# One feed-forward slab in a scratch place, the narrow layer's split halves in other places, and the fourth graph layer's logits ahead of its low halves

## The chip, the cores and the metric

The kernel runs as one program on one core of a Trainium2 chip. The metric is the device time of one execution in microseconds. The engines are PE (matrix products), DVE and ACT (elementwise work), POOL, and SP, which issues nearly all loads of weights.

## The reference

The input is 128 nodes of 768 numbers and 2048 edges. Eight blocks follow each other, each adding to its input what it computes from a normalised copy:

```
x = x + L0_gnn(layernorm(x))   # attention over edges: 8 heads x 768, then 1 x 768
x = x + L0_ffn(layernorm(x))   # tokens split by a router: self-attention or mixing; then a 48-wide net
x = x + L1_gnn(layernorm(x))   # 8 heads x 128, relu, then 1 x 768
x = x + L1_ffn(layernorm(x))   # mixture: 8 experts + 1 shared, 1536 wide, 2 chosen per token
x = x + L2_gnn(layernorm(x))   # 12 heads x 64
x = x + L2_ffn(layernorm(x))   # 8 experts, 48 wide
x = x + L3_gnn(layernorm(x))   # 4 heads x 512, elu, then 1 x 768
x = x + L3_ffn(layernorm(x))   # mixture: 8 experts, 3072 wide, 2 chosen per token
```

A graph layer projects x, forms for each edge a logit from two terms per head, takes a softmax over each node's incoming edges, and sums the projected neighbours by it.

## The kernel before

**Slabs and places.** All large weights lie in memory as slabs of 128 x 3072 numbers (1.5 MB). SP issues one load a slab (L596), in a fixed order, into one of 15 places: six in `ring` (0 to 5), six in `scratch` (6 to 11), three in `extra` (12 to 14). The table `SLOT` says which slab goes where; until the first mixture it is the slab's number modulo 6, after that the place that is given up first. Before each load SP waits (`room`) for the semaphore that tells that the place's former slab is used up (`when_used`). SP is one queue: a load that waits holds up all behind it.

**The slabs around the change.** Slabs 24 to 31 belong to L0_ffn: in order the weights of keys, queries, values, mixing (to 29) and attention output (four of its six tiles in 30, two in 31), and in 31 also those of the 48-wide net. 32 to 35 are the four slabs of the L1 graph layer (`c` = 2 in the code, the "narrow" layer), and 36 onward are the first mixture's: nine for the shared expert, then those of the chosen experts, which SP can only address once the router has written their order (`sid`, L634). The first nine of the second mixture are loaded ahead of its router in the same way.

**Split products.** Most weights are multiplied as a rounded high half and a rest: ACT writes the high half (`narrow_split_hi`, `graph_split_hi`), DVE subtracts it (`narrow_split_lo`, `graph_split_lo`), each in two pieces of 128 x 1536, and PE multiplies both. ACT and DVE run their instructions in the order in which the program has them.

**The stretch of L0_ffn.** PE forms the logits of self-attention; DVE takes their maximum (`self_max`); ACT takes exponentials (L993); DVE normalises (`self_weights`); PE transposes (L2235), runs two more parts of the mixing product (L2209), and multiplies by the values (L2243); ACT copies the context (L1001); PE forms `attn_out` (L2252), which ends in `merged` (L2258).

**The narrow layer.** Two segments of 512 columns pass through `project`, `term_rows`, `logits`, `weights_of`, `turn_attention`, `attend`, `activate`, `turn_segment` (L1779) and `product2` (L1811), with step t of each engine's loop `first_narrow(2)` working on different segments at once.

**The fourth graph layer** (`c` = 5) runs the same loop over four segments. POOL loads its attention vectors (`vectors`) when an earlier pair of vectors has been used, and `terms` on DVE waits for them. Ahead of it, in L2_ffn, ACT takes a Gelu (L1039) of PE's product L2333, and DVE weights the result (L1614).

Of the kernel before, what the change touches and what calls it, by code (L numbers as in the profile page):

```python
# [19 lines left out]
RING = 6  # L20
# [36 lines left out]
FFN0_SLAB = 24  # L57
# [116 lines left out]
for k, s in enumerate(slots_in_turn(1, [0, 1, 14, 2, 7, 3, 8, 4, 9, 6, 5, 12])):  # L174
    SLOT[MOE[1]["slab"] + k] = s
# [131 lines left out]
def gnn_ffn_kernel(nc, x_in, edges_in, weights, rows_in, cols_in, small_in, attn_in, ffn0_vectors, l2_terms_in, out):  # L307
    with ExitStack() as ctx:
# [283 lines left out]
        def _(sp):  # L592
            sp.dma_start(X[:], x_in).then_inc(S("x_loaded"), 16)

            def slab(n, index):
                sp.dma_start(slab_at(n), weights[index]).then_inc(land[SLOT[n]], 16)  # L596
# [54 lines left out]
            for n in range(MOE[1]["slab"]):  # L651
                room(n)
                slab(n, n)
# [82 lines left out]
        def _(act):  # L736
# [131 lines left out]
            def first_narrow(c):  # L868

                n = FIRST[c]["segs"]  # L870
                for t in range(n + 3):
                    if c == 2 and t < 2:
                        narrow_split_hi(t + 2)
# [115 lines left out]
            narrow_split_hi(0)  # L989
# [5 lines left out]
            ins.then_inc(S("self_exps"), 1)  # L995
            act.wait_ge(S("self_turned"), 1)
            A(ALT[:, 0:3 * P], TP[:, 0:3 * P], ACT.Copy).then_inc(S("self_attn_ready"), 1)
            act.wait_ge(S("places_turned"), 1)
            A(placesT, MS[:, 2 * P:3 * P], ACT.Copy).then_inc(S("places_ready"), 1)
            act.wait_ge(S("context"), 1)  # L1000
# [7 lines left out]
            narrow_split_hi(1, (1,))  # L1008
            transposed(3)
            act.wait_ge(S("f_product"), 1)  # L1010
            A(FT[0:F0, :], MS[0:F0, 0:P], ACT.Gelu, bias=cols[0:F0, 14:15]).then_inc(S("f_ready"), 1)

# [24 lines left out]
            graph_split_hi(1)  # L1037
# [4 lines left out]
            A(CBT[0:E8, :], TP[0:E8, SEG:SEG + P], ACT.Copy).then_inc(S("l2_T_ready"), 1)  # L1042
            keep_x(6)
# [10 lines left out]
        def _(dve):  # L1054
# [259 lines left out]
            def first_narrow(c):  # L1314
                n, k, C = FIRST[c]["segs"], GAT[c]["group"], GAT[c]["C"]
                for t in range(n + 2):
                    if c == 5 and t == 5:
                        graph_segment_lo(2)
                    if c == 2 and t == 0:
                        narrow_split_lo(2)  # L1320
                    if c == 2 and t == 2:
                        narrow_split_lo(3, (0,))
                    if c == 5 and t < 3:
                        graph_split_lo(*((2, (0,)), (3, (0,)), (3, (1,)))[t])
                    if 0 <= t - 1 < n:
                        logits(c, t - 1)
                    if t < n:
                        dve.wait_ge(S("h_copied"), SEG_BASE[c] + t + 1)
                        terms(GAT[c]["unit"] + t, range(t * k, t * k + k), C, h_tile(c, t))
                        if c == 5 and t == 0:  # L1330
                            graph_split_lo(2, (1,))
# [5 lines left out]
                    if c == 2 and t == 2:  # L1337
                        narrow_split_lo(3, (1,))
# [247 lines left out]
            narrow_split_lo(1, (1,))  # L1586

# [890 lines left out]
```

## Time and profile before

| | before |
|---|---|
| time of the runs | 1204.87 us median of 3 (1202.83 to 1208.21) |
| time of the profiled execution | 1205.36 us |
| its span, first to last instruction | 1203.6 us |
| PE busy | 1142.2 us (95%) |
| DVE busy | 581.8 us (48%) |
| ACT busy | 458.5 us (38%) |
| bytes moved by DMA | 443.15 MB, mean 368 GB/s |
| mean granted clock of PE | 0.994 |

The span runs from the first instruction to the last; the time of an execution holds 1.8 us around it. Busy shares are means over stages with different limits. The granted clock is a share of full speed (2.4 GHz).

### The profile page before, as it was taken

What the parts mean: (1) busy time and instruction counts of PE and PEld (TensorE: products, weight loads), DVE (VectorE), ACT (ScalarE), POOL (GpSimd) and SP (SyncE); (2) the same over time, 40 slices, a digit from 0 to 9 for tenths busy, and PEclk for the clock granted to TensorE, in tenths of its full rate; (3) what the DMA queues carried; (4) which work ended last, traced back from release to release, by engine and by line L of the source; (5) the groups of instructions that cost most, each with busy time, mean ns of one, the idle gap of its engine ahead of it and who ended that gap; (6) DMA issues with size and microseconds to landing.
All of it is one profiled execution on the core that took longest, in us unless ns stands there. A gap on an engine that the chain in (4) does not pass through costs nothing.

```text
span 1203.6 us, 15702 instructions
## 1 busy us (share of the span) xinstructions
PE 1142.2 (95%) x6347; PEld 721.7 (60%) x6347; DVE 581.8 (48%) x892; ACT 458.5 (38%) x525; POOL 22.4 (2%) x48
## 2 busy tenths in 40 slices
PE   8899998989999999989999999999999999889988
PEld 6677784767855455535866686565665655445533
DVE  7877742747644234301665684454554543223410
ACT  4755613515633223201444364343443432222210
POOL 2000010000000000000000000000000000000000
PEclk9999999989999999999999999999999999999999
DMA  9998564864999999999786298999999999999997
GB/s 372 423 407 344 199 246 180 337 266 192 426 425 426 424 425 425 426 420 419 290 311 260 82 428 337 427 425 427 425 424 425 426 426 424 425 426 425 425 423 285
DMA packets 45368, 443.15 MB, mean 368 GB/s; under 512 B 5088, under 2 KB 5248, under 8 KB 11888
## 3 DMA queue, kind: packets, MB, share of 16 engines
q1 hardware_dynamic: 42336, 427.05, 85.5%
q0 software_dynamic: 2960, 15.09, 3.3%
q8 instruction: 51, 0.84, 0.3%
q14 instruction: 21, 0.17, 0.0%
HBM read 441.73 MB, written 0.39 MB: 367 GB/s over the span
## 4 chain that ended last, share of the span: by engine, by line
PE 70%; DMA 14%; ACT 5%; SPq 5%; DVE 4%; issue 1%; POOL 0%; DVEq 0%; ACTq 0%
PE PJ L2036 14%; PE PJ L2005 10%; DMA scratch<-in_weights 9%; PE AC L2073 8%; PE TP L2095 6%; PE PJ L2014 5%; DMA ring<-in_weights 5%; SPq L647 4%; PE AC L1832 3%; PE AC L1820 2%; PE PJ L1996 2%; PE TP L2046 2%; PE MS L1633 1%; PE PJ L1766 1%; PE AC L1811 1%
## 5 line engine op out<-in xcount | busy, mean ns | idle before, releaser
L2036 PE MATMUL PJ<-ring,picked 128*64 128x512 f32 (+1 forms) x588 | 149.7, 594 | 0.0
L915 ACT ACTIVATE low<-PJ 128x512 f32<-128x512 f32 x51 | 30.3, 593 | 242.8 <-PE PJ L2036 170.2
L1391 DVE SCALAR_TENSOR_TENSOR act<-low,CB,PJ 128x512 f32<-128x512 f32 x51 | 38.0, 746 | 159.4 <-PE PJ L2005 84.1
L2036 PE MATMUL PJ<-scratch,picked 128*32 128x512 f32 (+1 forms) x360 | 106.9, 594 | 2.2 <-DMA extra<-in_weights 2.2
L2095 PE MATMUL TP<-ring,extra 128*64 128x512 f32 (+3 forms) x384 | 102.5, 488 | 2.8 <-issue 2.4
L1409 DVE TENSOR_TENSOR ring_lo<-ring,w_lo_u 128x1536 fp32r<-128x1536 f32 x40 | 69.2, 1756 | 52.4 <-ACT w_lo_u L932 52.4
L2095 PE MATMUL TP<-scratch,extra 128*64 128x512 f32 (+3 forms) x320 | 86.5, 489 | 0.4 <-DMA ring<-in_weights 0.4
L932 ACT ACTIVATE w_lo_u<-ring 128x1536 fp32r<-128x1536 f32 x40 | 58.3, 1487 | 66.6 <-DMA ring<-in_weights 30.2
L2036 PEld LDWEIGHTS PJ<-ring,picked 128*64 128x64 f32 (+1 forms) x588 | 42.7, 124 | 55.6 <-issue 54.9
L1409 DVE TENSOR_TENSOR ring_lo<-ring,w_hi_u 128x1536 fp32r<-128x1536 f32 x34 | 58.9, 1755 | 23.4 <-ACT w_hi_u L932 23.2
L2014 PE MATMUL PJ<-ring_lo,XTh 128*128 128x512 f32 x168 | 67.2, 400 | 0.0
L932 ACT ACTIVATE w_hi_u<-scratch 128x1536 fp32r<-128x1536 f32 x26 | 37.5, 1482 | 77.6 <-DMA scratch<-in_weights 61.8
L2095 PE MATMUL TP<-extra 128*64 128x256 f32 (+3 forms) x256 | 64.4, 488 | 0.9 <-issue 0.9
L932 ACT ACTIVATE w_hi_u<-ring 128x1536 fp32r<-128x1536 f32 x34 | 49.7, 1487 | 29.9 <-PE AC L2073 20.1
L2005 PE MATMUL PJ<-w_lo_u,extra_lo 128*128 128x512 f32 x150 | 60.6, 404 | 0.0
L2005 PE MATMUL PJ<-w_hi_u,extra_lo 128*128 128x512 f32 x150 | 58.9, 403 | 1.7 <-DVE extra_lo L1409 1.7
L2005 PE MATMUL PJ<-w_lo_u,XTh 128*128 128x512 f32 x150 | 59.2, 395 | 0.0
L2005 PE MATMUL PJ<-w_hi_u,XTh 128*128 128x512 f32 x150 | 59.2, 394 | 0.0
L2095 PEld LDWEIGHTS TP<-ring,extra 128*64 128x64 f32 (+1 forms) x384 | 38.2, 124 | 34.4 <-issue 29.1
L2036 PE MATMUL PJ<-extra,picked 128*32 128x512 f32 (+1 forms) x204 | 58.9, 594 | 0.0
L2036 PE MATMUL PJ<-ring,extra 128*64 128x512 f32 x156 | 53.5, 595 | 3.0 <-DMA ring<-in_weights 2.2
L2073 PE MATMUL AC<-w_hi_u,extra_lo 128*128 128x512 f32 x208 | 48.9, 348 | 6.0 <-DVE extra_lo L1417 6.0
(467 smaller groups left out, 2256.0 us busy)
## 6 DMA issues: line engine op xcount, KB each, us to landing
ring<-in_weights SPq DMA_DIRECT2D x147, 1536.0 KB, 17.6
scratch<-in_weights SPq DMA_DIRECT2D x73, 1536.0 KB, 19.6
extra<-in_weights SPq DMA_DIRECT2D x39, 1536.0 KB, 20.7
extra<-in_attn POOLq DMA_DIRECT2D x11, 768.0 KB, 10.7
ring<-in_weights SPq DMA_DIRECT2D x8, 768.0 KB, 30.1
extra<-in_attn POOLq DMA_DIRECT2D x6, 512.0 KB, 10.7
extra<-in_weights SPq DMA_DIRECT2D x4, 768.0 KB, 25.7
ring<-in_weights SPq DMA_DIRECT2D x8, 384.0 KB, 16.8
```

The source lines that it names most:

```text
L647: sp.dma_start(slab_at(of)[:, part], weights[index, :, part]) \
L915: A(silu, PJ[:, 0:SEG], ACT.Silu).then_inc(S("silu_ready"), 1)
L932: A(hi_half(n, half), half_slab(n, half), ACT.Copy).then_inc(S("whole_hi"), 1)
L1391: v.scalar_tensor_tensor(hexp, silu, weight, PJ[:, SEG:2 * SEG], ALU.mult, ALU.mult) \
L1409: v.tensor_tensor(slab_lo(n)[:, half * HALF:(half + 1) * HALF], half_slab(n, half), hi_half(n, half).bitcast(F32), ALU.subtract).then_inc( ...
L1820: ins = mm(AC[:, a:b], act1T[:, j % 2, t * P:(t + 1) * P], slab_at(n)[:, t * D + a:t * D + b], start=(j == 0 and t == 0), stop=(j == last ...
L1832: ins = mm(AC[:, a:b], x[:, t * P:(t + 1) * P], w[:, t % 2 * D + a:t % 2 * D + b], start=(j == 0 and t == 0 and x is xl), stop=False, skip ...
L2005: return mm(dst, x[:, t, :], hi_half(n, t // 3)[:, t % 3 * SEG:(t % 3 + 1) * SEG], start=start, stop=stop)
L2014: mm(dst, XTh[:, t, :], slab_lo(n)[:, t * SEG:(t + 1) * SEG], start=(apart and t == 0), stop=False)
L2036: ins = mm(dst[c], x[:, t, c], slab_at(LOAD[q, kind, side])[:, t * SEG:(t + 1) * SEG], start=(t == 0), stop=(t == KT - 1))
L2073: ins = mm(AC[:, a:b], x[:, t * P:(t + 1) * P], w[:, a:b], start=False, stop=(q == end and t == 3 and w is hi and x is hTh), skip_group_ch ...
L2095: ins = mm(Y[c, a:b], hT_of(q)[:, t * P:(t + 1) * P][:, c], slab_at(LOAD[q, "d", side])[:, t * D + a:t * D + b], start=(j == j0 and t == 0 ...
```

## The change

The kernel's diff has four parts. First, slab 30 (`CONTEXT_SLAB`) goes to place 6, the first sixth of `scratch`, which the first graph layer gives up when its last segment has been multiplied (`segment_product` at 12). The slabs behind it move back by one place: 31 to place 0, 32 to 1, 33 to 2, 34 to 3, 35 to 4, 36 to 5. So SP now waits before slab 31 for `k_product` (before: `q_product`), before 32 for `q_product` (as before), before 33 for `q_product` (before: `v_product`), before 34 for `v_product` (before: `merged`), and before 35 for `merged` (as before). The first mixture takes up its places in another opening order, since place 5 is now in its list first; the events that its loads wait for are the same, under other place numbers. Of the slabs 117 to 126, behind it, slabs 118, 120, 122 and 124 now wait for the next later of the last passes' products.

Second, ACT's narrow high halves stand elsewhere: slab 32's halves behind the exponentials, slab 34's halves inside L0_ffn (before: in the narrow layer). Third, DVE's low halves of slabs 34 and 35 stand earlier by up to two steps. Fourth, one high half of slab 120 moves behind ACT's Gelu, and in the fourth graph layer the two low halves of its fourth slab stand behind `logits`.

```diff
@@ -171,7 +171,11 @@
 
 
 SLOT = {n: n % RING for n in range(MOE[1]["slab"])}
-for k, s in enumerate(slots_in_turn(1, [0, 1, 14, 2, 7, 3, 8, 4, 9, 6, 5, 12])):
+CONTEXT_SLAB = FFN0_SLAB + 6
+SLOT[CONTEXT_SLAB] = 6
+for n in range(CONTEXT_SLAB + 1, MOE[1]["slab"]):
+    SLOT[n] = (n - 1) % RING
+for k, s in enumerate(slots_in_turn(1, [5, 0, 1, 14, 2, 7, 3, 8, 4, 9, 6, 12])):
     SLOT[MOE[1]["slab"] + k] = s
 free = []
 for n in range(L2_SLAB - 1, MOE[1]["slab"], -1):
@@ -650,6 +654,8 @@
 
             for n in range(MOE[1]["slab"]):
                 room(n)
+                if n == CONTEXT_SLAB:
+                    sp.wait_ge(S("segment_product"), FIRST[0]["segs"])
                 slab(n, n)
             mixture(1, (8, 9), 14, 12)
             for n in range(L2_SLAB, MOE[3]["slab"]):
@@ -869,8 +875,8 @@
 
                 n = FIRST[c]["segs"]
                 for t in range(n + 3):
-                    if c == 2 and t < 2:
-                        narrow_split_hi(t + 2)
+                    if c == 2 and t == 0:
+                        narrow_split_hi(3)
                     if c == 5 and t < 2:
                         graph_split_hi(t + 2, (0,))
                     if t < n:
@@ -986,17 +992,18 @@
             ins.then_inc(S("mix_ready"), 1)
             act.wait_ge(S("v_product"), 1)
             A(V, AC[:, 0:D], ACT.Copy).then_inc(S("v_ready"), 1)
-            narrow_split_hi(0)
             act.wait_ge(S("self_max"), 1)
             for r, s, at in ((slice(0, P), 0, SEG), (slice(0, P), 1, 2 * SEG), (slice(0, DH), 2, SEG + P),
                              (slice(DH, P), 2, 2 * SEG + P)):
                 ins = A(EE[r, s * P:(s + 1) * P], TP[r, at:at + P], ACT.Exp, bias=hneg[r, s:s + 1], scale=DH ** -0.5,
                         accum_out=hsum[r, s:s + 1])
             ins.then_inc(S("self_exps"), 1)
+            narrow_split_hi(0, (0,))
             act.wait_ge(S("self_turned"), 1)
             A(ALT[:, 0:3 * P], TP[:, 0:3 * P], ACT.Copy).then_inc(S("self_attn_ready"), 1)
             act.wait_ge(S("places_turned"), 1)
             A(placesT, MS[:, 2 * P:3 * P], ACT.Copy).then_inc(S("places_ready"), 1)
+            narrow_split_hi(0, (1,))
             act.wait_ge(S("context"), 1)
             A(contextT.rearrange("p k n -> p (k n)"), AC[:, 0:D // 4], ACT.Copy).then_inc(S("context_ready"), 1)
             narrow_split_hi(1, (0,))
@@ -1006,9 +1013,11 @@
                 r = slice(c * BLOCK, (c + 1) * BLOCK)
                 A(spread[r, c * (D // 4):(c + 1) * (D // 4)], MS[r, 0:D // 4], ACT.Copy).then_inc(S("spread_made"), 1)
             narrow_split_hi(1, (1,))
+            narrow_split_hi(2, (0,))
             transposed(3)
             act.wait_ge(S("f_product"), 1)
             A(FT[0:F0, :], MS[0:F0, 0:P], ACT.Gelu, bias=cols[0:F0, 14:15]).then_inc(S("f_ready"), 1)
+            narrow_split_hi(2, (1,))
 
             keep_x(2)
             transposed(4, XTh[:])
@@ -1034,12 +1043,13 @@
             transposed(7)
             act.wait_ge(S("pe_d"), LAST_PASS[1] + 1)
             graph_split_hi(0)
-            graph_split_hi(1)
+            graph_split_hi(1, (0,))
             act.wait_ge(S("l2_hidden_product"), 1)
             A(G2, PJ[:, 0:E8 * F2], ACT.Gelu).then_inc(S("l2_gelu"), 1)
             act.wait_ge(S("l2_turned"), 1)
             A(G2T, TP[:, 0:E8 * F2], ACT.Copy).then_inc(S("l2_T_ready"), 1)
             A(CBT[0:E8, :], TP[0:E8, SEG:SEG + P], ACT.Copy).then_inc(S("l2_T_ready"), 1)
+            graph_split_hi(1, (1,))
             keep_x(6)
 
             transposed(8, XTh[:])
@@ -1317,13 +1327,16 @@
                     if c == 5 and t == 5:
                         graph_segment_lo(2)
                     if c == 2 and t == 0:
-                        narrow_split_lo(2)
-                    if c == 2 and t == 2:
+                        narrow_split_lo(2, (1,))
                         narrow_split_lo(3, (0,))
-                    if c == 5 and t < 3:
-                        graph_split_lo(*((2, (0,)), (3, (0,)), (3, (1,)))[t])
+                    if c == 2 and t == 1:
+                        narrow_split_lo(3, (1,))
+                    if c == 5 and t == 0:
+                        graph_split_lo(2, (0,))
                     if 0 <= t - 1 < n:
                         logits(c, t - 1)
+                    if c == 5 and 1 <= t < 3:
+                        graph_split_lo(3, (t - 1,))
                     if t < n:
                         dve.wait_ge(S("h_copied"), SEG_BASE[c] + t + 1)
                         terms(GAT[c]["unit"] + t, range(t * k, t * k + k), C, h_tile(c, t))
@@ -1334,8 +1347,6 @@
                         narrow_segment_lo(t - 2)
                     if 0 <= t - 1 < n:
                         weights_of(c, t - 1)
-                    if c == 2 and t == 2:
-                        narrow_split_lo(3, (1,))
                     if 0 <= t - 2 and FIRST[c]["elu"]:
                         activate(c, t - 2)
                     if c == 5 and 3 <= t < 5:
@@ -1584,6 +1595,7 @@
             dve.wait_ge(S("h1_ready"), 1)
             layernorm_affine(2, H1[:], vec(3), vec(4))
             narrow_split_lo(1, (1,))
+            narrow_split_lo(2, (0,))
 
             layernorm(3, X[:], 5, 2)
             transposed_lo(4, XT_lo, "graph_tokens_lo")
```

On ACT, in L0_ffn, from the copy of the values (`scratch<-AC 128x768`) to the activation that ends L0_ffn, the rows before are these. L865 is a high half of a narrow slab (`extra_lo` is slab 32's, `w_lo_d` slab 33's, `w_hi_g` slab 34's), L993 the exponentials, L997 to L1007 the copies of attention, places, context and output.

```order
L988 ACTIVATE scratch<-AC 128x768
L865 ACTIVATE extra_lo<-ring 128x1536 x2
L993 ACT_TABLE_LOAD
L993 ACTIVATE scratch,hsum<-TP,hneg 128x128 x2
L993 ACTIVATE scratch,hsum<-TP,hneg 64x128 x2
L997 ACTIVATE scratch<-TP 128x384
L999 ACTIVATE scratch<-MS 128x128
L1001 ACTIVATE scratch<-AC 128x192
L865 ACTIVATE w_lo_d<-ring 128x1536
L1007 ACTIVATE scratch<-MS 32x192 x2
L865 ACTIVATE w_lo_d<-ring 128x1536
L743 ACTIVATE extra<-TP 128x384 x2
```

And in the change, where L871 is the high half and L998 the exponentials:

```order
L994 ACTIVATE scratch<-AC 128x768
L998 ACT_TABLE_LOAD
L998 ACTIVATE scratch,hsum<-TP,hneg 128x128 x2
L998 ACTIVATE scratch,hsum<-TP,hneg 64x128 x2
L871 ACTIVATE extra_lo<-ring 128x1536
L1003 ACTIVATE scratch<-TP 128x384
L1005 ACTIVATE scratch<-MS 128x128
L871 ACTIVATE extra_lo<-ring 128x1536
L1008 ACTIVATE scratch<-AC 128x192
L871 ACTIVATE w_lo_d<-ring 128x1536
L1014 ACTIVATE scratch<-MS 32x192 x2
L871 ACTIVATE w_lo_d<-ring 128x1536
```

Slab 32's two halves stand behind the exponentials, one of them ahead of the copies and one behind, and the next row of the change is slab 34's first half.

On DVE, in the narrow layer's third step (t = 2), L1166 to L1169 normalise the weights of segment 0, L1240 is the first low half of slab 35, and L1147 opens the logits of segment 1. Before:

```order
L1166 TENSOR_SCALAR hsum<-hsum 128x4
L1168 RECIPROCAL hrec<-hsum 128x4
L1169 TENSOR_TENSOR scratch<-scratch,hrec 128x512
L1240 TENSOR_TENSOR ring_lo<-ring,w_lo_g 128x1536
L1147 ISA scratch,hmax<-TP,maskb 128x128
L1147 ISA hmax 128x1
```

And in the change, where L1176 to L1179 and L1157 are the same lines:

```order
L1176 TENSOR_SCALAR hsum<-hsum 128x4
L1178 RECIPROCAL hrec<-hsum 128x4
L1179 TENSOR_TENSOR scratch<-scratch,hrec 128x512
L1157 ISA scratch,hmax<-TP,maskb 128x128
L1157 ISA hmax 128x1
```

The low half (`ring_lo<-ring,w_lo_g`) no longer stands between the two; it stands at the loop's first and second step.

On ACT, in L2_ffn, L859 writes the high halves of slabs 119 (`w_hi_u`) and 120 (`w_lo_u`), L1039 is the Gelu, and L1041 and L1042 copy its transposed result. Before:

```order
L743 ACTIVATE extra<-TP 128x384 x2
L859 ACTIVATE w_hi_u<-ring 128x1536 x2
L859 ACTIVATE w_lo_u<-scratch 128x1536 x2
L1039 ACT_TABLE_LOAD
L1039 ACTIVATE scratch<-PJ 128x384
L1041 ACTIVATE scratch<-TP 128x384
L1042 ACTIVATE scratch<-TP 8x128
```

And in the change, where L865 is the high half and L1048 the Gelu:

```order
L749 ACTIVATE extra<-TP 128x384 x2
L865 ACTIVATE w_hi_u<-ring 128x1536 x2
L865 ACTIVATE w_lo_u<-scratch 128x1536
L1048 ACT_TABLE_LOAD
L1048 ACTIVATE scratch<-PJ 128x384
L1050 ACTIVATE scratch<-TP 128x384
L1051 ACTIVATE scratch<-TP 8x128
L865 ACTIVATE w_lo_u<-scratch 128x1536
```

Slab 120's second half has moved from ahead of the Gelu to behind the copies.

## Rows read from the trace of the kernel before

**Rows 1.** The page: 40 slices of 30.1 us; shares of the last chain.
```profile
GB/s 372 423 407 344 199 246 180 337 266 192 426 425 426 424 425 425 426 420 419 290 311 260 82 428 337 427 425 427 425 424 425 426 426 424 425 426 425 425 423 285
...
PE 70%; DMA 14%; ACT 5%; SPq 5%; DVE 4%; issue 1%; POOL 0%; DVEq 0%; ACTq 0%
```

**Rows 2.** Waits of SP's DMA queue: us, times, longest.
```profile
SPq L634 <- DVE sid L1435: 52.9, 2, 31.2
```

**Rows 3.** Timeline of SP's queue: start, us, instruction.
```profile
262.63 23.48 SPq L596 DMA_DIRECT2D scratch<-in_weights  x2
...
684.36 0.88 SPq L596 DMA_DIRECT2D ring<-in_weights  x2
```

**Rows 4.** Timeline of ACT: start, us, instruction [idle before <- releaser].
```profile
168.11 1.28 ACT L977 ACT_TABLE_LOAD   x1
...
194.20 2.86 ACT L865 ACTIVATE extra_lo<-ring 128x1536 fp32r<-128x1536 f32 x2 [1.95 <-DMA ring<-in_weights]
197.07 1.28 ACT L993 ACT_TABLE_LOAD   x1
```

**Rows 5.** Timeline of DVE, 193 to 201.
```profile
193.16 0.17 DVE L1570 TENSOR_SCALAR hneg<-hmax 128x3 f32<-128x3 f32 x1
200.01 0.18 DVE L1572 RECIPROCAL hrec<-hsum 128x3 f32<-128x3 f32 x1 [6.69 <-ACT scratch L993]
```

**Rows 6.** Timeline of PE, 191 to 207.
```profile
191.94 4.14 PE L2209 MATMUL PJ<-ring,scratch 128*128 128x512 f32 x12
...
200.84 0.90 PE L2235 MATMUL TP<-ident,scratch 128*128 128x128 f32 x3 [4.65 <-DVE scratch L1573]
201.53 3.96 PE L2209 MATMUL PJ<-ring,scratch 128*128 128x512 f32 x8
```

**Rows 7.** Landings: slabs 31 (issued 181.6), 32 (182.0), vector loads (150.9, 151.4).
```profile
DMA to landing us min/median/max: 8.5/8.5/8.5
DMA to landing us min/median/max: 12.2/12.2/12.2
DMA to landing us min/median/max: 8.8/11.3/13.8
```

**Rows 8.** Windows: width, busy by engine, PEclk, DMA share, GB/s.
```profile
201.00:204.00 3.00, 3.00 (x7) 1.88 (x8) 3.00 (x2) 0.66 (x2) 0.00 (x0) 0.51 0.02 5
245.20:251.40 6.20, 5.51 (x18) 4.43 (x19) 4.25 (x13) 1.18 (x3) 0.00 (x0) 0.50 0.53 223
256.00:261.00 5.00, 3.58 (x21) 2.98 (x22) 1.28 (x2) 0.60 (x1) 0.00 (x0) 1.00 1.01 430
```

**Rows 9.** The chain by time, narrow layer: start, us, what.
```profile
240.95 1.67 DVE ring_lo L1240
...
244.47 0.60 DVE act L1184
...
246.92 6.66 PE AC L1811 x24
...
258.05 4.52 PE AC L1811 x24
```

**Rows 10.** Timeline of PE, 242 to 246.
```profile
242.35 1.16 PE L1766 MATMUL PJ<-scratch 128*128 128x128 f32 x8 [0.26 <-ACT scratch L790]
245.11 1.12 PE L1779 MATMUL MS<-ident,act 128*128 128x128 f32 x4 [1.61 <-DVE act L1184]
```

**Rows 11.** Timeline of ACT, at 599.
```profile
598.81 1.28 ACT L1039 ACT_TABLE_LOAD   x1
```

**Rows 12.** Timeline of DVE, 596 to 631.
```profile
596.58 3.43 DVE L1225 TENSOR_TENSOR ring_lo<-ring,w_hi_u 128x1536 fp32r<-128x1536 f32 x2
600.63 0.56 DVE L1614 TENSOR_TENSOR scratch<-scratch,extra 128x384 f32<-128x384 f32 x1 [0.62 <-ACT scratch L1039]
...
630.60 0.69 DVE L1128 CUSTOM_DVE_ANT_0 extra<-scratch,extra 128x512 f32<-128x512 f32 x1 [1.00 <-DMA extra<-in_attn]
```

**Rows 13.** Timeline of PE, 595 to 599.
```profile
594.97 4.14 PE L2333 MATMUL PJ<-ring,extra 128*128 128x384 f32 x12
```

## The prediction

> **What bounds the kernel now.** I read the page first. Its slices of 30.1 us show weights streaming at about 425 GB/s from 300 to 570 us and, but for one slice, from 690 us to the last; between 90 and 300, and again between 570 and 690, the rate is 82 to 344 GB/s [rows 1]. The chain that ended last runs mostly over PE (70%), but that is because products free the places for loads; at full rate the bytes set the pace. The waits of SP's queue then say why a stream starts when it does: it stood 52.9 us in two waits for the order of the experts [rows 2], that is for each mixture's router. Both streams start from an idle DMA: the slices holding the two waits have 192 and 82 GB/s [rows 1]. So what the compute ahead of a router gains moves the whole stream behind it, PE with it, and the end. Nothing that changes inside a mixture is part of this change: the loads wait for the same products there, under other place numbers. The first load past the order goes out at 262.63 + 23.48 = 286.1 in the first mixture and at 684.4 in the second [rows 3]. So the sum is made of what is gained ahead of 286, and between the first mixture's last product and 684.
>
> **L0_ffn.** DVE has the maximum at 193.16 + 0.17 = 193.33 [rows 5], but ACT waits for slab 32 to land until 194.20, writes its high halves until 197.06, loads the exponential's table for 1.28 [rows 4], and its exponentials end at about 200.0, where DVE's reciprocal starts [rows 5]. PE, whose work before ended 4.65 earlier, resumes at 200.84 [rows 6]. In the change the table load comes right behind the copy of the values. ACT was idle for 1.95 before 194.20 [rows 4], so it is free at 192.25, the table is in at 193.53, and everything up to PE's transposes comes 197.07 + 1.28 - 193.53 = 4.8 earlier. PE itself is busy until 200.84 - 4.65 = 196.19, so 4.65 is the gain, and the gap closes.
>
> That gap also cost clock. In the window behind it the granted clock is 0.51, the lower level of 1.2 GHz [rows 8]; three transposes take 0.69 to the next start there and eight products of the mixing weight 3.96. At the upper level, 2.4 GHz, twelve such products take 4.14 [rows 6], so eight take 2.76, and the transposes half of theirs, 0.35: a gain of 1.2 + 0.35, of which I take 1.5. **L0_ffn: 4.65 + 1.5 = 6.15 less.**
>
> What must hide: half of slab 32's high half (1.43, half of 2.86) stands between the exponentials (then ending at 195.2) and the copy of attention. That copy is queued behind it, and PE waits for the copy only after its eight products, at about 199.3; so slab 32 may land as late as 197 at no cost. It is third in the queue now and took 12.2 from 182.0, to 194.2; in the change it is second, as slab 31 now, which took 8.5 from 181.6, to 190.1 [rows 7]. Behind it, slabs 33 and 34 take the turns of 32 and 33. The halves of 34 that now stand in L0_ffn (three pieces, two on ACT and one on DVE) fall into stretches where these engines wait for PE; if that cover were gone, each would cost its 1.4 to 1.8.
>
> Slab 30 now loads earlier, beside the vector loads of L0_ffn, the later of which is issued at 151.4 and lands 13.8 later, at 165.2 [rows 7]. ACT's table load for the router's sigmoid waits for it and stood at 168.11 [rows 4]. 1.57 MB at 425 GB/s are 3.7, so it could land at 168.9 at worst: 0 to +0.8. I take 0, since slab 30 queues behind another slab and shares only the last part.
>
> **The narrow layer.** The chain has DVE write a low half from 240.95 for 1.67, then the logits, then the activation at 244.47 [rows 9]. Without that half the logits can end 1.67 earlier, but the activation also waits for the product L1766, which ends at 242.35 + 1.16 = 243.51 [rows 10]. It starts at about 243.6: **-0.85**, and PE's wait before L1779 shrinks from 1.61 [rows 10] to about 0.75. The half itself moves to DVE's wait for PE ahead of the first logits; were there no wait, 1.67 would come back.
>
> From that wait on the clock is 0.50 until 251.4 [rows 8]: four transposes take 1.12 [rows 10], and the following product 6.66 against 4.52 for its like at full clock [rows 9]. If the clock holds, 0.55 and 2.15 are gained: **-2.7**; if it falls again, 0. I take -2.7: the stretch at 256 to 261, with PE busy 3.58 of 5.00, keeps 1.00 [rows 8], and it holds the same sequence of product, activation and transposes for the other segment, with shorter waits, which is what the change makes of the first.
>
> The Trainium skill speaks against that certainty ("TensorE: Matmul & The Clock Gate", Part 1): the clock is reduced by default and released by activity, judged in windows that run free of the program, so that a gap's effect depends on where it falls. Of the two low stretches here each follows a wait of PE, which agrees; by the rule a shorter gap may still be caught, the sum would lack 2.7, and that is rival A below.
>
> **L2_ffn and the fourth graph layer.** ACT writes two slabs' high halves and then loads the Gelu's table at 598.81 [rows 11]. One half less (1.43, as above) lets the load start at 597.4. The Gelu then waits for PE's product, which ends at 594.97 + 4.14 = 599.1 [rows 13], and DVE's weighting, at 600.63, for a low half that ends at 596.58 + 3.43 = 600.0 [rows 12]: **-0.6**, with a bound of 0 (if the table load stays behind) and -1.4. In the fourth graph layer the logits come one half (1.7) earlier, but the third `terms` starts at 630.60 on the landing of a vector load [rows 12], which is triggered by earlier `terms` that don't move. What the half gives back before is waited for there: **0** (bounds: 0 and -1.7, a half's length). The half that is now later has to be ready for PE's fourth projection; DVE's wait of 1.00 before 630.60 [rows 12] is there for it.
>
> Slabs 118, 120, 122 and 124 wait for a later product, but load while the stream drains and are needed after 590: 0.
>
> **Sum:** 6.15 + 0.85 + 2.7 + 0.6 = 10.3. The profiled execution took 1205.4 with a span of 1203.6, and stands 0.5 above the median of the runs (1204.9). **Prediction: 1195.0 us.**
>
> **The rivals.**
> A. The clock falls again in the narrow layer. For it: the wait there doesn't vanish. Then 10.3 - 2.7 = 7.6, 1197.8 us.
> B. Only L0_ffn's gain arrives; narrow layer and L2_ffn are held by something that the chain doesn't show (ACT's exponentials, a landing), and the change doesn't do there what it says. For it: both gains are small differences of ends that lie close together. Then 6.15, 1199.2.
> C. ACT's queue is held by slab 32. Its first half now stands ahead of the copy of attention; each microsecond that it lands past 197 is one of the path. It takes back all at a landing at 207.3 and makes the kernel 6 slower (1211) at 213. Against it: the longest of the landings in that stretch, as third in the queue, was 12.2 [rows 7]; here it would have to be 31.
> D. The gain ahead of the first router is lost in the mixture: 1204 at most. Against it: the DMA is idle before the wait ends [rows 1, 2].
>
> **How the numbers follow.** Forecast 0.60, A 0.20, B 0.11, D 0.05, C 0.04. What separates this kernel from no change is about 0.5%, 6 us, since its runs spread from 1202.8 to 1208.2. Forecast and A lie below 1198.8, so does B in half of its cases: faster 0.84. D and B's other half: same 0.12. C: slower 0.04. The range: below, -10.3 with 1.7 more in the fourth graph layer and 0.8 in L2_ffn, and the spread of runs, 1191.5; above, past B with 0.8 for the vector load, 1200.5. It leaves out C, D and the ends, under 2 in 10.
>
> **What would show it.** PE's wait of 4.65 gone and `self_exps` ahead of slab 32's halves; the granted clock at 1.00 from 190 to 260; L1811 twice at about 4.5; the first router's order about 9.7 earlier, at 276; the end of the first mixture as much; the Gelu's result 0.6 nearer to the mixture's end; the third `terms` still waiting for the vector load. The prediction is wrong if the first stream starts 9.7 earlier but doesn't end so, or if a new wait of ACT for a landing stands in L0_ffn.

## The result, and the profile after

The changed kernel took 1196.96 us (median of 4 runs, 1195.55 to 1199.68), the kernel before 1204.7 beside it (4 runs, 1202.83 to 1208.21): a ratio of 0.9935, 95% interval 0.9906 to 0.9964. Two more comparisons of the same two kernels, among the experiments below, give 1196.91 to 1206.7 (ratio 0.992, 0.9897 to 0.9944) and 1195.67 to 1205.31 (0.9925, 0.9908 to 0.9943). So it is faster by 0.65 to 0.8%, 7.7 to 9.8 us. Forecast were 10.3 and 1195.0, range 1191.5 to 1200.5. The profiled execution took 1199.68 with a span of 1197.9; of its four runs it is the slowest.

L0_ffn first. PE's timeline in the changed kernel, from the mixing product to the merged one (start, us, instruction, idle before):

```profile
192.03 4.14 PE L2221 MATMUL PJ<-ring,scratch 128*128 128x512 f32 x12
196.01 0.27 PE L2244 MATMUL MS<-ident,scratch 128*128 128x128 f32 x1
196.12 0.55 PE L2247 MATMUL TP<-ident,scratch 128*128 128x128 f32 x3
196.50 2.75 PE L2221 MATMUL PJ<-ring,scratch 128*128 128x512 f32 x8
...
204.74 1.53 PE L2270 MATMUL PJ<-scratch 128*128 128x512 f32 x4 [0.96 <-DVE scratch L1590]
```

L2247 are the transposes that waited 4.65 before [rows 6]: no wait stands there now, they take 0.55 for 0.90, and the eight products behind them 2.75 for 3.96. ACT's timeline shows why:

```profile
192.35 1.28 ACT L998 ACT_TABLE_LOAD   x1
...
195.28 1.49 ACT L871 ACTIVATE extra_lo<-ring 128x1536 fp32r<-128x1536 f32 x1
196.79 0.49 ACT L1003 ACTIVATE scratch<-TP 128x384 f32<-128x384 f32 x1
197.18 0.27 ACT L1005 ACTIVATE scratch<-MS 128x128 f32<-128x128 f32 x1
197.34 1.49 ACT L871 ACTIVATE extra_lo<-ring 128x1536 fp32r<-128x1536 f32 x1
```

The table load starts 4.7 earlier than in [rows 4], and slab 32's halves fill ACT's time behind the exponentials without a wait for a landing. The chain of the narrow layer in order of time comes next, then PE's wait in it, then windows (width, five busy times, PE's granted clock, DMA share, GB/s):

```profile
237.29 0.70 DVE act L1194
237.99 0.04 issue
238.04 0.67 PE MS L1791 x4
...
239.38 4.51 PE AC L1823 x24
...
248.36 4.51 PE AC L1823 x24
```

PE's wait ahead of the four transposes at 238.04 is 0.79, for 1.61 before [rows 10]:

```profile
238.04 0.66 PE L1791 MATMUL MS<-ident,act 128*128 128x128 f32 x4 [0.79 <-DVE act L1194]
```

```profile
201.00:204.00 3.00, 2.78 (x51) 1.65 (x49) 0.15 (x1) 1.04 (x2) 0.00 (x0) 1.00 0.00 0
238.00:245.00 7.00, 6.03 (x33) 4.74 (x33) 2.58 (x12) 1.20 (x2) 0.00 (x0) 1.00 0.70 276
245.00:252.00 7.00, 5.42 (x32) 4.55 (x33) 1.38 (x2) 0.60 (x1) 0.00 (x0) 1.00 0.92 388
...
528.00:532.00 4.00, 4.00 (x14) 1.43 (x12) 0.00 (x0) 0.00 (x0) 0.00 (x0) 0.57 1.02 418
586.00:590.00 4.00, 4.00 (x8) 2.19 (x8) 3.76 (x10) 3.90 (x3) 0.00 (x0) 0.57 0.00 0
```

The first of the two equal products took 6.66 before [rows 9] and takes 4.51 now; the low clock of [rows 8] is gone from both places. But two other places have one, 528 and 586, where the profiled execution of before had 1.00. SP's timeline has the two ends that the prediction named, the first loads past the routers' orders:

```profile
276.06 0.94 SPq L600 DMA_DIRECT2D scratch<-in_weights  x2
...
676.82 0.88 SPq L600 DMA_DIRECT2D ring<-in_weights  x2
```

Past the first order the load goes out 9.7 earlier than in the profiled execution of before (whose row in [rows 3] covers two loads; the second is at 285.76), as forecast. Past the second it is 7.5 earlier [rows 3], and the spans differ by 5.7 only. SP's waits for the orders are as long as they were [rows 2]:

```profile
SPq L638 <- DVE sid L1446: 53.0, 2, 31.2
```

So the mechanism came as predicted, and in this execution 4 of the 9.7 went astray behind 276. The experiments ask which of the steps ahead of 276 carry the gain, and whether the change lost those 4 or chance did.

### The profile page after: what moved, and what is told of

Its sections match the earlier page's. It is cut to its first block, busy times and chain, and to the rows that moved or that the text cites. A ratio compares the mean times of both kernels' runs of the same rounds, so it can differ in the third digit from the quotient of the medians.

```text
span 1197.9 us, 15702 instructions
## 1 busy us (share of the span) xinstructions
PE 1142.2 (95%) x6347; PEld 721.3 (60%) x6347; DVE 582.3 (49%) x892; ACT 458.3 (38%) x525; POOL 22.4 (2%) x48
## 4 chain that ended last, share of the span: by engine, by line
PE 73%; DMA 16%; ACT 4%; DVE 3%; SPq 3%; issue 1%; POOL 0%; DVEq 0%; ACTq 0%
PE PJ L2048 14%; PE PJ L2017 10%; DMA scratch<-in_weights 8%; PE AC L2085 8%; PE TP L2107 7%; PE PJ L2026 5%; DMA ring<-in_weights 4%; PE AC L1844 3%; DMA extra<-in_weights 3%; PE AC L1832 2%; SPq L651 2%; PE PJ L2008 2%; PE MS L1645 2%; PE TP L2058 2%; PE PJ L1778 1%
## 5 line engine op out<-in xcount | busy, mean ns | idle before, releaser
L2048 PE MATMUL PJ<-ring,picked 128*32 128x512 f32 (+1 forms) x612 | 160.4, 594 | 0.0
L2048 PE MATMUL PJ<-scratch,picked 128*64 128x512 f32 (+1 forms) x336 | 113.9, 600 | 2.2 <-DMA extra<-in_weights 2.2
L1420 DVE TENSOR_TENSOR ring_lo<-ring,w_lo_u 128x1536 fp32r<-128x1536 f32 x44 | 76.1, 1755 | 69.1 <-ACT w_lo_u L938 69.1
L2107 PE MATMUL TP<-ring,extra 128*64 128x512 f32 (+2 forms) x464 | 102.1, 488 | 0.9 <-issue 0.9
L2048 PEld LDWEIGHTS PJ<-ring,picked 128*32 128x32 f32 (+1 forms) x612 | 45.8, 123 | 58.6 <-issue 57.4
L938 ACT ACTIVATE w_hi_u<-scratch 128x1536 fp32r<-128x1536 f32 x30 | 43.5, 1483 | 76.5 <-DMA scratch<-in_weights 53.1
L2107 PE MATMUL TP<-extra 128*64 128x512 f32 (+2 forms) x224 | 64.3, 488 | 0.0
L2107 PEld LDWEIGHTS TP<-ring,extra 128*32 128x32 f32 (+1 forms) x464 | 38.9, 123 | 35.5 <-issue 30.6
L1420 DVE TENSOR_TENSOR ring_lo<-ring,w_hi_u 128x1536 fp32r<-128x1536 f32 x28 | 48.4, 1756 | 21.8 <-ACT w_hi_u L938 21.5
L938 ACT ACTIVATE w_hi_u<-ring 128x1536 fp32r<-128x1536 f32 x28 | 40.6, 1486 | 33.2 <-PE AC L2085 17.2
```

The costliest lines, as they stand in the source:

```text
L938: A(hi_half(n, half), half_slab(n, half), ACT.Copy).then_inc(S("whole_hi"), 1)
L1420: v.tensor_tensor(slab_lo(n)[:, half * HALF:(half + 1) * HALF], half_slab(n, half), hi_half(n, half).bitcast(F32), ALU.subtract).then_inc( ...
L2048: ins = mm(dst[c], x[:, t, c], slab_at(LOAD[q, kind, side])[:, t * SEG:(t + 1) * SEG], start=(t == 0), stop=(t == KT - 1))
L2107: ins = mm(Y[c, a:b], hT_of(q)[:, t * P:(t + 1) * P][:, c], slab_at(LOAD[q, "d", side])[:, t * D + a:t * D + b], start=(j == j0 and t == 0 ...
```

## The experiments

**Theory:** what the change gains ahead of the first order moves everything behind it; what is missing behind 276 are falls of the clock and delays of transfers that differ from one execution to the next, whatever the kernel. **Rival:** the change pays behind 550, by other places, the moved half of slab 120 and later waits; then the losses recur in each execution of it.

Below, "the order" is the order of the experts that a router writes, and a "fall" is a stretch in which the granted clock is at the lower level, 0.50 of full speed; a window that holds more than the fall shows a mean between 0.50 and 1.00.

All traces are set side by side in this table, worked out from PE's and SP's rows of each: end of the merged product (L0_ffn); from there to the first load past the first order (narrow layer and router); to the product that opens L2_gnn (mixture 1); the hidden product of L2_ffn; from its end to the transposes behind the Gelu; from there to the first load past the second order (the last of L2_ffn, fourth graph layer, router); from there to the end (mixture 2). The stretch between mixture 1 and the hidden product is left out: 32.35 to 32.61 in all.

| trace | merged ends | narrow | mixture 1 | hidden | to transposes | graph 4 | mixture 2 | span |
|---|---|---|---|---|---|---|---|---|
| before | 212.51 | 73.25 | 276.84 | 4.14 | 2.14 | 83.12 | 519.2 | 1203.6 |
| before_again | 211.61 | 72.15 | 278.01 | 5.49 | 1.17 | 84.38 | 519.4 | 1204.8 |
| narrow_warm | 212.44 | 71.70 | 277.76 | 5.52 | 1.17 | 84.39 | 520.8 | 1206.4 |
| order_only | 206.90 | 72.15 | 276.90 | 5.83 | 1.17 | 82.97 | 520.3 | 1198.6 |
| slots_only | 209.04 | 69.81 | 276.98 | 4.14 | 1.43 | 82.69 | 519.9 | 1196.3 |
| lo_at_2 | 206.39 | 71.89 | 277.70 | 5.53 | 1.17 | 82.68 | 521.0 | 1199.0 |
| no_l2 | 206.02 | 69.77 | 277.73 | 4.14 | 2.13 | 84.40 | 519.0 | 1195.6 |
| after | 206.27 | 69.79 | 277.74 | 5.83 | 1.17 | 83.65 | 521.1 | 1197.9 |
| after_again | 206.37 | 69.78 | 276.71 | 4.14 | 1.43 | 84.33 | 519.4 | 1194.5 |
| after_third | 206.26 | 69.76 | 276.84 | 4.14 | 1.43 | 82.79 | 520.0 | 1193.6 |
| warm_more | 206.47 | 69.77 | 277.07 | 4.14 | 1.43 | 83.36 | 521.2 | 1195.8 |

**after_again and before_again: both kernels once more.** No edit.

> The changed kernel once more, for a second trace. Theory (a shift that chance events eat into): the first load past the first router's order again at 276 us and the last product of the first mixture 9 to 10 earlier than before, but the stretches of low granted clock stand elsewhere than at 528, 586, 1078 and 1146, and the span differs from 1197.9 by 2 to 4. Median 1196 to 1197. Rival (the change itself costs something behind 550: other places, the moved half, other products): the low stretches and the losses of 0.9, 0.7, 0.5 and 1.8 stand at the same places again, span 1197.5 to 1198.5.

> The kernel before once more, for a second trace. Forecast's reason (the low clock at 245 to 251 follows from the wait of 1.6 there): the granted clock is 0.50 there again, the product behind it takes 6.7, the first load past the router's order goes out at 286. Rival (the fall is chance): the clock holds, the product takes 4.5, the order is known 2.7 earlier, at 283, and 2.7 of the change's gain isn't the change's.

The changed kernel: 1196.91 (6 runs, 1196.28 to 1199.41), order at 276.15, span 1194.5. The clock held where it had fallen, and fell at 616 to 622 instead:

```profile
586.00:590.00 4.00, 4.00 (x13) 2.25 (x12) 3.86 (x6) 3.45 (x4) 0.00 (x0) 1.00 0.00 0
528.00:532.00 4.00, 4.00 (x20) 1.38 (x16) 0.00 (x0) 0.00 (x0) 0.00 (x0) 1.00 1.02 418
616.00:622.00 6.00, 5.66 (x16) 3.47 (x16) 4.97 (x18) 3.30 (x6) 0.87 (x2) 0.72 0.94 376
```

The kernel before took 1206.61 in its one run. Its clock fell in the narrow layer again, but for less of it:

```profile
201.00:204.00 3.00, 3.00 (x7) 1.52 (x5) 2.09 (x2) 0.05 (x1) 0.00 (x0) 0.53 0.03 5
244.00:252.00 8.00, 7.09 (x33) 5.87 (x33) 4.41 (x14) 1.49 (x5) 0.00 (x0) 0.79 0.45 189
```

The order came at 283.76 and not 285.76: 1.1 from the shorter fall, and 0.9 since slab 32 landed earlier, which ACT's row shows (194.20 in [rows 4]):

```profile
193.18 2.86 ACT L865 ACTIVATE extra_lo<-ring 128x1536 fp32r<-128x1536 f32 x2 [1.18 <-DMA ring<-in_weights]
```

283.76 is near the rival's 283, but the rival's condition, a clock that holds, was not met.

For the rival's losses: in the table mixture 1 is 1 longer in 5 traces, of both kernels, each with a fall that starts between 526.9 and 535.9; so it is with the hidden product (1.4 to 1.7 longer), again in both. None of these losses comes back in each execution of the changed kernel, so the rival falls.

**order_only: the order on ACT alone**, on the kernel before, all places as before.

```diff
-            narrow_split_hi(0)
             act.wait_ge(S("self_max"), 1)
...
             ins.then_inc(S("self_exps"), 1)
+            narrow_split_hi(0, (0,))
...
             A(placesT, MS[:, 2 * P:3 * P], ACT.Copy).then_inc(S("places_ready"), 1)
+            narrow_split_hi(0, (1,))
```

> The kernel before with one edit: slab 32's high halves behind the exponentials, all places as before. Theory: the order alone does it, since slab 32 lands at 194.2 and its half is wanted at 195.2: PE's wait of 4.65 is gone, the merged product ends 6.2 earlier, the first order 6.2 earlier (279.6) if the narrow layer's wait stays as it was; median 1198 to 1199. Rival (the place is needed, the half waits for a landing): the first order within 2 us of 286, median over 1202.

1199.83 (6 runs, 1199.02 to 1201.82; ratio 0.9942, 0.9919 to 0.9965). PE has no wait ahead of the transposes, and ACT none ahead of slab 32's first half:

```profile
196.64 0.27 PE L2233 MATMUL MS<-ident,scratch 128*128 128x128 f32 x1
196.75 0.55 PE L2236 MATMUL TP<-ident,scratch 128*128 128x128 f32 x3
```

```profile
195.91 1.49 ACT L865 ACTIVATE extra_lo<-ring 128x1536 fp32r<-128x1536 f32 x1
```

The merged product ends 4.7 to 5.6 earlier than in the three traces with the old order, and L0_ffn started 0.6 later here (the mixing product at 192.67 for 192.03), behind a fall at 46.7 that the other traces lack. The narrow layer keeps its wait of 1.60 and a fall of the clock (72.15):

```profile
239.51 0.66 PE L1780 MATMUL MS<-ident,act 128*128 128x128 f32 x4 [1.60 <-DVE act L1185]
```

The order on ACT carries all of L0_ffn's gain.

**slots_only: the places alone.** The changed kernel with that edit undone.

```diff
             ins.then_inc(S("self_exps"), 1)
-            narrow_split_hi(0, (0,))
...
+            narrow_split_hi(0)
             act.wait_ge(S("self_max"), 1)
```

> The changed kernel with slab 32's high halves back ahead of the exponentials; the places stay changed. Theory (the order carries the gain, the place does little for it): slab 32 lands at 190.0, ACT writes its halves from 192.25 to 195.1, the table load ends at 196.4 and the exponentials at 198.1 instead of 195.2; PE waits 2.9 again, the clock may fall behind it as before (1.5), and the first load past the first router's order goes out at 279 to 280.5 instead of 276.1; median 3 to 4.4 above the changed kernel's. Rival (the earlier landing is what gives the gain): no wait of PE, 276 to 277, median within 1.

1199.13 (6 runs, 1198.16 to 1200.99; ratio 0.9935, 0.9919 to 0.9951). ACT no longer waits for the slab, but its halves still stand ahead of the table load, and PE waits 2.58:

```profile
192.26 2.85 ACT L871 ACTIVATE extra_lo<-ring 128x1536 fp32r<-128x1536 f32 x2
195.12 1.28 ACT L999 ACT_TABLE_LOAD   x1
```

```profile
198.89 0.55 PE L2246 MATMUL TP<-ident,scratch 128*128 128x128 f32 x3 [2.58 <-DVE scratch L1583]
```

The first load past the order goes out at 278.86, 2.8 behind the changed kernel's: the exponentials' delay, and no fall of the clock behind this shorter wait. What the places give, by the traces, is slab 34 early (landed at 200.3 in after, at 219.1 in before), so that three of its four halves can leave the narrow layer. That is argued and not shown: no run takes back the places alone.

**lo_at_2: slab 35's low halves back at the third step**, on the changed kernel.

```diff
-                        narrow_split_lo(3, (0,))
-                    if c == 2 and t == 1:
-                        narrow_split_lo(3, (1,))
+                    if c == 2 and t == 2:
+                        narrow_split_lo(3, (0,))
...
                         weights_of(c, t - 1)
+                    if c == 2 and t == 2:
+                        narrow_split_lo(3, (1,))
```

> The changed kernel with slab 35's low halves back at the narrow loop's third step. Forecast's reason (logits later by a half and a wait long enough for the clock to fall): the activation 0.85 later, PE's wait about 1.6, the product behind it at 6.6 instead of 4.5, the first load past the order at 276.1 + 0.85 + 2.7 = 279.6, median 3.5 above the changed kernel's. Rival (the clock falls by chance, not by that wait): 0.85 alone, 276.9, median 0.9 above.

1198.91 (6 runs, 1198.17 to 1200.78), 2.0 above after_again in the same comparison; ratio 0.9931, 0.9908 to 0.9953. The wait of 1.6 is back, the transposes start 0.81 later behind the merged product (238.97 - 206.39 against 238.04 - 206.27), and the clock falls:

```profile
238.97 0.66 PE L1792 MATMUL MS<-ident,act 128*128 128x128 f32 x4 [1.60 <-DVE act L1194]
```

```profile
236.00:244.00 8.00, 5.50 (x25) 4.62 (x26) 6.45 (x26) 2.03 (x6) 0.00 (x0) 0.79 0.79 335
```

The order is 2.2 later (278.28): 0.8 by the wait, 1.3 by the clock, for which 2.7 stood in the expectation. Between the theories it decides for the forecast's reason, at half its size.

**narrow_warm: the clock alone.** The kernel before, with fills in PE's wait.

```diff
                     if 0 <= t - 3 < n:
+                        if n == 2 and t == 3:
+                            keep_warm(13)
                         turn_segment(c, t - 3)
```

> The kernel before with 13 products of the identity, whose result nobody reads, in PE's wait of 1.6 ahead of the narrow layer's first transposes. Theory (the clock falls there because PE stands idle): the granted clock stays 1.00 from 245 to 252, the four transposes take 0.66 and the first product 4.5, the activation is as late as before, and the first load past the order goes out 2.7 earlier, at 283.1; median 2 to 3 below the kernel before. Rival (the fall is chance or follows from something else): 0.50 stands there again, 284 to 286, and the median is that of before.

The clock held, the product took 4.5, and the fills (two rows for each product) ended 1.1 behind the activation:

```profile
243.25 3.07 PE L1633 MATMUL MS<-ident 128*128 128x128 f32 x26
246.16 0.60 PE L1779 MATMUL MS<-ident,act 128*128 128x128 f32 x4
```

```profile
244.00:252.00 8.00, 7.31 (x51) 6.50 (x51) 5.18 (x17) 1.87 (x5) 0.00 (x0) 1.00 0.57 239
```

Narrow takes 71.70, so 70.6 but for the fills' delay; 2.65 less than in the first trace of before, 1.55 less than in the second. The time, 1206.14 (12 runs, 1202.54 to 1208.29; ratio 0.9987, 0.9971 to 1.0002), shows no sure gain, where 2 to 3 were expected: of the 1.55 to 2.65 that the fills win they give back 1.1.

**no_l2: without the fourth part.**

```diff
             graph_split_hi(0)
-            graph_split_hi(1, (0,))
+            graph_split_hi(1)
...
-            graph_split_hi(1, (1,))
...
-                    if c == 5 and t == 0:
-                        graph_split_lo(2, (0,))
+                    if c == 5 and t < 3:
+                        graph_split_lo(*((2, (0,)), (3, (0,)), (3, (1,)))[t])
                     if 0 <= t - 1 < n:
                         logits(c, t - 1)
-                    if c == 5 and 1 <= t < 3:
-                        graph_split_lo(3, (t - 1,))
```

> The changed kernel without its fourth part (both high halves of slab 120 ahead of the Gelu, the fourth graph layer's low halves ahead of its logits). Theory: from the end of the hidden product to PE's next transposes 2.1 again instead of 1.2, so 0.9 later from there on; in the fourth graph layer nothing, since its third terms wait for the vector load in either order; median 0.9 above the changed kernel's. Rival (the part is without effect, or harmful through the moved halves): 1.2 stays or is given back before the second router's order; median the same or lower.

1197.57 (6 runs, 1196.81 to 1199.3; ratio 0.9922, 0.9906 to 0.9938). ACT's table load ends behind the hidden product again, and PE waits:

```profile
585.88 4.14 PE L2342 MATMUL PJ<-ring,extra 128*128 128x384 f32 x12
592.15 0.55 PE L2349 MATMUL TP<-ident,scratch 128*128 128x128 f32 x3 [0.84 <-DVE scratch L1623]
```

```profile
589.72 1.28 ACT L1048 ACT_TABLE_LOAD   x1
591.01 0.49 ACT L1048 ACTIVATE scratch<-PJ 128x384 f32<-128x384 f32 x1
```

From the hidden product to the transposes 2.13, for 1.43 in the changed kernel: the part gives 0.7. But only where the clock holds in that product. Where it falls, the product ends so late that ACT's halves are done in any order, and the step is 1.17 with the part (after) and without it (before_again). In the fourth graph layer the stage takes 84.40 here and 84.33 in after_again, both with a fall there.

**warm_more and after_third: more fills, beside the changed kernel.**

```diff
+                    if n == 4 and t == 2:
+                        keep_warm(3)
                     if 0 <= t - 1 < n:
                         if n > 2 or t > 1:
                             term_rows(c, t - 1)
+                        if n == 4 and t == 2:
+                            keep_warm(1)
...
+            keep_warm(3)
             attend_l2(2).then_inc(S("x_product"), 1)
...
-            turn(7, XN, warm=15)
+            turn(7, XN, warm=16)
```

> The changed kernel with 8 more products of the identity, whose result nobody reads, in PE's short waits: 4 ahead of the transposes before the mixture-free net's gate product (L2_ffn), 4 around the fourth graph layer's second term rows. Theory (at these two places PE is idle just enough for the clock to fall in about half of the executions): the granted clock stays 1.00 in the hidden product (4.14) and at the fourth graph layer's second attention; from the transposes behind the Gelu to the second router's order 83.2 instead of 84.9; median 0.5 to 1.5 below the changed kernel run beside it. Rival (those falls don't follow from the waits): as often as before; the fills cost up to 0.5; median the same or a little above.

> The changed kernel a third time, beside the one with more fills. Theory: the first load past the first router's order at 275.7 to 276.2 for the third time; each stretch behind it as long as in one of the two former traces, by whether the clock falls in it (first mixture up to L2_gnn 276.7 or 277.7, Gelu's transposes 1.4 or 1.2 behind the hidden product); median 1196.5 to 1197.5. Rival: another order of events at the first router, over 1 us from 276.1.

1196.08 with fills (5 runs, 1195.41 to 1198.32) and 1195.67 without (6 runs, 1195.22 to 1199.43): no difference. In both traces the clock held at both places, so that they don't say what the fills do; a theory of falls by half needs more executions. The order of the changed kernel came at 276.02 the third time, as expected; its median is 0.8 below the expected 1196.5 to 1197.5.

**code_more: what made mixture 2 longer by 1.8.** In the traces each load announces its arrival in 16 updates. Their distances hardly change from one load to the next, which is read here as one update from each of the 16 DMA engines. The distances from the first, for the same load late in mixture 2 (first arrival, then 16 distances in us, worked out from the traces):

```
before       1157.41  0.0 0.0 0.0 0.6 0.8 1.0 2.2 2.4 2.9 3.0 3.5 3.6 3.7 4.8 4.8  5.7
after        1149.93  0.0 0.1 0.4 0.5 0.7 1.2 1.3 2.5 3.2 3.5 3.6 3.7 3.8 5.1 5.5  7.4
after_again  1148.77  0.0 0.2 0.4 0.5 0.5 1.1 1.1 2.4 2.9 3.0 3.0 3.1 3.2 3.5 5.1  5.2
code_more    1148.86  0.0 0.1 0.2 0.3 0.9 1.1 1.9 2.8 3.3 3.4 3.8 3.8 4.0 4.2 6.0 25.4
```

The first engine is 7.5 ahead of before in the trace of after, the last only 5.7. These lags grow in steps; one of 1.6, on the last engine of after, falls between two loads at 767, just behind a packet that carries instructions (at 764.6). The page counts 51 such packets of 16 KB in either kernel. So this kernel adds instructions:

```diff
             ln_power(8)
+            for _ in range(16384):
+                pool.wait_ge(S("ln_rstd"), 9)
```

> The changed kernel with some 8200 more instructions on POOL (waits that are already met), behind its last work, beside the second mixture: 0.5 MB of instructions, 64 packets of 8 KB at 0.31 us. Theory (packets that carry instructions take turns on the DMA engines of the weights' stream, and the engine that is behind sets the end): spread evenly 4 packets or 1.2 to 1.8 us for each of the 16 engines, more on the last, so the span is 1 to 3 longer and the last landing of the stream that much later. Rival (those packets cost the stream nothing): the span is as in the changed kernel, 1194 to 1198.

The queues of DMA in the stretch 690 to 1190 (packets, MB, share of 16 engines), of this kernel and of after_again, and SP's issue of the output here:

```profile
q8 instruction: 21, 0.34, 0.3%
q14 instruction: 49, 0.40, 0.2%
```

```profile
q8 instruction: 22, 0.36, 0.3%
q14 instruction: 7, 0.06, 0.0%
```

```profile
1213.81 0.82 SPq L667 DMA_DIRECT2D out<-extra  x2
```

By the updates, the additional packets all went to one engine: its lag rose from 3.0 at 772 to 25.4 at 1149, while 38 packets of 8 KB passed, 0.6 each, and the others' stayed as they were. The output is issued 22.1 later than in after_again (1191.70), not 1 to 3: the theory's mechanism, without the even spread. The time of 1395.03 (4 runs; ratio 1.1553) says nothing more, since POOL goes through the rest of its waits alone until then.

## Why the prediction was right

**L0_ffn, 6.15.** Measured 6.24 in the profiled pair, and 5.3 to 6.2 against the other traces of before. Wait, table load and clock came as worked out, and order_only shows that it is the order on ACT. The vector load that was given 0 to 0.8 landed 15.6 behind its issue for 13.8 [rows 7] and cost nothing: ACT's table load stands at 168.20, for 168.11 [rows 4].

**Narrow layer, 0.85 and 2.7.** The first measured 0.81. The second is the term that was mis-sized: 2.65 in the profiled execution, 1.3 to 1.6 in the three others with that wait (before_again, order_only, lo_at_2), since the fall lasts less there (the granted clock is 0.50 over 6.2 us in [rows 8], 0.79 over 8 us in before_again and lo_at_2). That idle time of PE causes it is shown: the clock fell in all four traces with a wait of 1.6 and in none of the seven with 0.8 (code_more among them), nor with the wait filled. Its length alone does not decide, though: the wait of 2.58 in slots_only, at another place, was followed by no fall. The Trainium skill ("TensorE: Matmul & The Clock Gate", Part 1) says that the windows by which the clock is set run free of the program, so that where the clock changes depends on where in a window the products fall. For rival A that was taken as a chance that the shorter wait is still caught. No trace here shows it caught; that the cost of the longer one varies between 1.3 and 2.65 agrees with that page.

**L2_ffn, 0.6.** 0.7 where the clock holds in the hidden product, 0 where it falls. The bound of 0 stood for another cause.

**Fourth graph layer, 0.** The third `terms` still waits for the vector load, longer than before [rows 12] in the trace of after and shorter in that of after_third:

```profile
623.05 0.69 DVE L1138 CUSTOM_DVE_ANT_0 extra<-scratch,extra 128x512 f32<-128x512 f32 x1 [1.59 <-DMA extra<-in_attn]
```

```profile
619.81 0.69 DVE L1138 CUSTOM_DVE_ANT_0 extra<-scratch,extra 128x512 f32<-128x512 f32 x1 [0.78 <-DMA extra<-in_attn]
```

What differs is how long that vector load takes from its issue to its landing, in the traces of before (issued at 620.74) and of after (issued at 612.66):

```profile
DMA to landing us min/median/max: 9.7/9.7/9.7
```

```profile
DMA to landing us min/median/max: 10.3/10.3/10.3
```

POOL issues it 19.5 behind the Gelu's transposes in all traces, and from the start of the third `terms` to the first load past the second order it is 53.75 to 53.80 in all seven traces without a fall there, with the part (slots_only, lo_at_2, after, after_third, warm_more) and without it (before, order_only). So the part gives nothing here, as forecast, and the landing sets the stage: 82.7 to 83.7 with the part, 83.0 to 83.1 without. Slabs 118 to 124 and the other places cost nothing that shows: mixture 1 takes 276.71 in the changed kernel (after_again) and 276.84 before, without a fall in either.

**The sum.** 9.7 was forecast at the first order and 9.7 is measured there, but against the trace that the forecast was made from, which has the longest fall in the narrow layer; against before_again the order comes 7.6 to 7.7 earlier. So the equal numbers are luck in part. The profiled pair then loses 0.9 in mixture 1 and 1.7 in the hidden product by the clock (1.0 comes back at the Gelu), 0.5 in the fourth graph layer by the vector load's landing and 1.8 in mixture 2: 9.7 - 0.9 - 1.7 + 1.0 - 0.5 - 1.8 = 5.8, for 5.7 between the spans. The clock's parts and mixture 2's occur in traces of either kernel. after_third, against the same trace of before, ends 10.0 earlier.

So the mechanism was right, and what failed in size is that the sum was made against one execution, as if the stages behind its terms took the same each time: each of four of them takes 1 to 2.2 more in some executions. By the median alone, rival A's 1197.8 fits 1196.96 and 1196.91 better than 1195.0 does, but its condition, a fall in the narrow layer, stands in no trace of the changed kernel. The prediction named as a sign of being wrong a first stream that doesn't end as much earlier as it starts. In the profiled pair it ends 8.8 earlier for 9.7, which is rival D in part, by the fall at 528; in after_again and after_third, without that fall, it ends 9.75 earlier. B and C didn't show.

Three figures of the prediction are slightly off without changing its argument. The row read as 286.1 covers two loads, the second issued at 285.76; 1205.4 - 10.3 is 1195.1; and forecast, A and half of B make 0.855, not 0.84.

## What to carry to other kernels

Ahead of a stream that starts on a result (here the order of the experts), each microsecond on the chain moves the whole stream: look there first, and at what an in-order engine does between two links of the chain that could as well stand behind. Cost a term by more than one execution, and compare stage by stage, before a difference of a few microseconds is put down to an edit. A wait of PE can cost more than its length: here one of 1.6 cost 1.3 to 2.65 more by the clock, and one of 0.8 nothing more.

## What was not expected of the hardware

Packets that carry instructions take their turn on the DMA engines that carry the weights, and where the stream is full, the delay stays: 0.6 for 8 KB (code_more), up to 1.6 for one of 16 KB (after). All of POOL's went to one engine, and in code_more that engine set the end of the stream. In the other traces this is only seen to go together: where the last engine lagged by over 7 at the end (after, narrow_warm, lo_at_2, warm_more), mixture 2 took 520.8 to 521.2, elsewhere, with 4.7 to 5.7, 519.0 to 520.3, and among these the lag does not order the times. The Trainium skill ("Runtime: NRT & Kernel Launch", "Instruction fetch mechanics") calls the cost of crossing a 16 KiB block of instructions mostly hidden. No run here measures that for the engine that fetches; for a stream that fills all DMA engines the 0.6 and 1.6 above are not hidden.

The clock also falls where PE hardly waits: in the hidden product, behind waits of 1.2 in all within 10 us, in 5 of the 11 traces of the table. What decides between two executions of the same instructions there stays open.
